# The decay mask of a recurrent attention kernel: its power computed in three pieces, and its semaphore waited for at the first use

## What is computed

```
q = xn @ Wq;  gate = softmax(xn @ Wg)
diff = s - t                                  # (512- to 1024-long causal pattern)
causal = diff > 0;  expn = max(diff - 1, 0)
for i in range(3):
    decay = sigmoid(decay_logits[i])          # logits 0, 3, 5
    w = decay ** expn * causal                # the decay mask
    scores = (q @ k_i.T) * w
    blended += gate[..., i] * (scores @ v_i)
y = x + (blended @ Wo * out_scale) * silu(ffn(xn))
```

## Time and profile before

| | |
|---|---|
| median of 3 runs | 1896.46 us (1894.89 to 1896.53) |
| the profiled execution's own time | 1895.22 us |
| its span, first to last instruction | 1893.2 us |
| mean granted clock of TensorE | 0.992 of full speed |
| busy, share of the span: TensorE, its weight loads | 97%, 66% |
| VectorE, GpSimd, ScalarE | 65%, 37%, 34% |
| chain that ended last | TensorE 92%, GpSimd 4%, the rest 1% or less each |

### The profile page before, as it was taken

How to read it: one execution, slowest core, us unless ns; L and a number is a source line. 1 busy time by engine, 2 the same in 40 slices (tenths; PEclk the granted TensorE clock), 3 DMA queues, 4 the chain that set the end, 5 groups by cost and what they waited for, 6 DMA issues and landing times.

```text
span 1893.2 us, 39454 instructions
## 1 busy us (share of the span) xinstructions
PE 1837.0 (97%) x14214; PEld 1249.3 (66%) x14214; DVE 1227.0 (65%) x2565; ACT 652.1 (34%) x1175; POOL 706.7 (37%) x641
## 2 busy tenths in 40 slices
PE   5786999999999999999999999999999999999999
PEld 1234848576685858677584857668585867758485
DVE  7773848576584838667484847658484856848374
ACT  2672414233332414243341423333242424334131
POOL 9393605234160614325060523416061432506021
PEclk9998999999999999999999999999999999999999
DMA  9962735566472746557373656647364654737350
GB/s 219 300 210 76 197 91 158 132 162 153 112 199 82 173 123 158 141 137 179 95 194 94 161 128 161 154 114 194 83 172 125 158 141 132 184 95 187 79 140 26
DMA packets 348662, 275.38 MB, mean 145 GB/s; under 512 B 216048, under 2 KB 253296, under 8 KB 348400
## 3 DMA queue, kind: packets, MB, share of 16 engines
q1 hardware_dynamic: 337664, 266.57, 53.7%
q0 software_dynamic: 10816, 6.30, 2.3%
HBM read 203.96 MB, written 30.54 MB: 124 GB/s over the span
## 4 chain that ended last, share of the span: by engine, by line
PE 92%; POOL 4%; DVE 1%; DMA 1%; issue 1%; SPq 1%; ACT 1%; POOLq 0%; DVEq 0%
PE F L1554 43%; PE F L1583 24%; PE B L1442 16%; POOL mask L668 3%; PE B L1474 2%; PE B L1447 2%; PE B L1449 2%; PE B L1448 2%; DVE region L1004 1%; PE F L1447 1%; PE F L1448 1%; PE F L1449 1%; DMA region<-in_wv 1%; SPq L519 0%; DMA lutrow<-in_lut 0%
## 5 line engine op out<-in xcount | busy, mean ns | idle before, releaser
L1554 PE MATMUL F<-xtc,ring 128*128 128x256 f16 (+1 forms) x4224 | 497.7, 273 | 0.0
L1554 PEld LDWEIGHTS F<-xtc,ring 128*128 128x128 f16 (+1 forms) x4224 | 416.0, 100 | 42.4
L1583 PE MATMUL F<-wd_hi,region 128*128 128x512 f16 (+1 forms) x1408 | 429.2, 379 | 0.0
L1554 PE MATMUL F<-xt,ring 128*128 128x256 f16 (+1 forms) x3168 | 378.8, 273 | 0.0
L1554 PEld LDWEIGHTS F<-xt,ring 128*128 128x128 f16 (+1 forms) x3168 | 309.9, 100 | 35.7 <-DVE region L1266 1.8
L1583 PE MATMUL F<-wd_lo,region 128*128 128x512 f16 (+1 forms) x704 | 266.7, 379 | 0.0
L1583 PEld LDWEIGHTS F<-wd_hi,region 128*128 128x128 f16 (+1 forms) x1408 | 137.5, 98 | 162.6
L684 POOL TENSOR_TENSOR rstd<-var,nhalf 128x4 f32<-128x4 f32 x15 | 15.3, 1019 | 595.3 <-DVE var L962 595.3
L1350 DVE SCALAR_TENSOR_TENSOR region<-F,row_out,region 128x512 f32<-128x512 f32 x64 | 48.0, 751 | 291.2 <-ACT region L931 291.2
L690 POOL TENSOR_TENSOR region<-region 128x512 f16<-128x512 f32 x96 | 121.6, 1267 | 220.9 <-ACT region L765 220.9
L931 ACT ACTIVATE region<-F,scale_hf 128x512 f32<-128x512 f32 x64 | 44.0, 687 | 435.5 <-PE F L1583 435.5
(11 more groups left out here) (200 smaller groups left out, 3069.9 us busy)
## 6 DMA issues: line engine op xcount, KB each, us to landing
ring<-blocks SPq DMA_DIRECT2D x546, 256.0 KB, 3.1
x_sb<-in_x SPq DMA_DIRECT2D x64, 256.0 KB, 3.5
out_y<-x_sb SPq DMA_DIRECT2D x64, 256.0 KB, 2.0
ring<-blocks SPq DMA_DIRECT2D x112, 128.0 KB, 2.5
blocks<-ring SPq DMA_DIRECT2D x35, 256.0 KB, 4.8
x_sb<-codes SPq DMA_DIRECT2D x10, 512.0 KB, 7.2
chalf<-codes SPq DMA_DIRECT2D x9, 512.0 KB, 7.1
xt<-codes SPq DMA_DIRECT2D x9, 512.0 KB, 9.0
```

The costliest lines, as they stand in the source:

```text
L1554: ins = T_.matmul(out_, a, b, start=fresh, stop=False, skip_group_check=True)
L1583: ins = T_.matmul(bf[:, :], a, b, start=(k == 0 and n == 0), stop=(k == FC - 1 and n == 2))
```

## The change

On GpSimd the iota and the maximum of the mask move up, directly behind `rstd`; the power over 128 x 384 becomes three powers over 128 x 128 (`power(0)`, `power(1)`, `power(2)`). The first stands in front of the sum over partitions, the other two behind the tables of powers. The wait for `s_dec` (the decays) moves up with the first. TensorE no longer waits for `s_mask`. VectorE waits for it in `probs_masked`, in front of every use, and no longer in front of its loop.

```diff
             pool.wait_ge(s_var, 2)
             G_.tensor_tensor(rstd[:, :], var[:, :], nhalf[:, :], ALU.pow).then_inc(s_rstd, 1)
-            pool.wait_ge(s_sq, 5)
-            G_.partition_all_reduce(gsum[:, :], amax[:, 0:5], P, RADD).then_inc(s_gsum, 1)
-
-            G_.iota(fade_s[:, :], ...)
-            G_.iota(fade_t[:, :], ...)
-            G_.memset(fade_tile[:, :], float(P)).then_inc(s_cstep, 1)
-            pool.wait_ge(s_dec, 3)
-            pool.wait_ge(s_cstep, 7)
-            for m in (fade_t, fade_s, fade_tile):
-                G_.tensor_tensor(m[:, :], decay[:, :], m[:, :], ALU.pow).then_inc(s_pow, 1)
...
             pool.wait_ge(s_mstep, 2)
             pool.wait_ge(s_pick, 2 * CG)
-            G_.tensor_tensor(mask[:, :, :], decay[:, :].unsqueeze(2).broadcast_to([P, NH, P]), mask_up,
-                             ALU.pow).then_inc(s_mstep, 1)
-            pool.wait_ge(s_mstep, 3)
+            pool.wait_ge(s_dec, 3)
+
+            def power(h):
+                G_.tensor_tensor(mask[:, h], decay[:, h:h + 1].broadcast_to([P, P]), mask_up[:, h],
+                                 ALU.pow).then_inc(s_mstep, 1)
+
+            power(0)
+            pool.wait_ge(s_sq, 5)
+            G_.partition_all_reduce(gsum[:, :], amax[:, 0:5], P, RADD).then_inc(s_gsum, 1)
+
+            G_.iota(fade_s[:, :], ...)
+            G_.iota(fade_t[:, :], ...)
+            G_.memset(fade_tile[:, :], float(P)).then_inc(s_cstep, 1)
+            pool.wait_ge(s_cstep, 7)
+            for m in (fade_t, fade_s, fade_tile):
+                G_.tensor_tensor(m[:, :], decay[:, :], m[:, :], ALU.pow).then_inc(s_pow, 1)
+
+            power(1)
+            power(2)
+            pool.wait_ge(s_mstep, 2 + NH)
             G_.affine_select(out=mask[:, :, :], in_=mask[:, :, :], compare_op=ALU.is_ge, fill=0.0,
                              **band).then_inc(s_mstep, 1)
...
             def probs_masked(gi, n):
 
+                dve.wait_ge(s_mask, 1)
                 dve.wait_ge(s_psc, gi * GT + n + 1)
...
-            dve.wait_ge(s_mask, 1)
             with dve.Fori(0, NB - 1) as i:
...
             pe.wait_ge(s_alo, len(MATS))
-            pe.wait_ge(s_mask, 1)
             with pe.Fori(0, NB - 1) as i:
```

More of the change, by code:

```diff
@@ L647, in _ @@
             G_.tensor_tensor(rstd[:, :], var[:, :], nhalf[:, :], ALU.pow).then_inc(s_rstd, 1)
+            band = dict(pattern=[[0, NH], [-1, P]], base=-1, channel_multiplier=1)
+            G_.iota(mask_up, allow_small_or_imprecise_dtypes=True, **band).then_inc(s_mstep, 1)
+            pool.wait_ge(s_mstep, 1)
+            G_.tensor_scalar(mask_up, mask_up, 0.0, None, ALU.max).then_inc(s_mstep, 1)
+            pool.wait_ge(s_mstep, 2)
+            pool.wait_ge(s_pick, 2 * CG)
+            pool.wait_ge(s_dec, 3)
[3 more added lines that the diff above has]
+            power(0)
             pool.wait_ge(s_sq, 5)
@@ L659, in _ @@
                 G_.tensor_tensor(m[:, :], decay[:, :], m[:, :], ALU.pow).then_inc(s_pow, 1)
[L662 to L667, removed]
-            G_.tensor_tensor(mask[:, :, :], decay[:, :].unsqueeze(2).broadcast_to([P, NH, P]), mask_up,
-                             ALU.pow).then_inc(s_mstep, 1)
-            pool.wait_ge(s_mstep, 3)
+            power(1)
+            power(2)
+            pool.wait_ge(s_mstep, 2 + NH)
             G_.affine_select(out=mask[:, :, :], in_=mask[:, :, :], compare_op=ALU.is_ge, fill=0.0,
                              **band).then_inc(s_mstep, 1)
-            pool.wait_ge(s_mstep, 4)
+            pool.wait_ge(s_mstep, 3 + NH)
             G_.tensor_scalar(mask[:, :, :], mask[:, :, :], 2.0 ** SP, None, ALU.mult).then_inc(s_mask, 1)
```

## The result

The changed kernel takes 1888.48 us, median of 5 runs (1887.88 to 1891.0); the kernel before 1896.53 in the same comparison. The ratio is 0.9959, 95% interval 0.9945 to 0.9974: faster by 8 us. The forecast was 1878.8 us, range 1875.5 to 1884: more than half of the gain that was forecast is missing. The profiled execution took 1887.88 us, its span is 1885.8.

A forecast was written before the change was run, and what follows sets the result against it. TensorE, 92% of the span, was taken to enter its loop late, waiting for GpSimd's mask. 18.15 - 2.2 (stall) + 1.7 (clock) = 17.65 us off 1895.22 gives 1877.6, as a median 1878.8; range 1875.5 to 1884.

The forecast's parts named there:

- TensorE's wait is removed: Entry of TensorE's loop: without the wait for the mask, the start moves from 156.46 to 138.31, by 18.15 us.
- The change of load in front of the sum: GpSimd, between power(0) and the sum over partitions: 8.3 us no longer hidden, so VectorE stalls 2.2 us.
- power(0): GpSimd's idle time behind `rstd`: the first power starts at 57.66, takes 21.1 us and ends at 78.8.
- The rival of unequal pieces: GpSimd's first power: head 0 might hold most of the 61.87 us, median up to 1919.6; chance 0.03.
- The rest of the mask: GpSimd behind the sum: tables 3.8 us as before, two powers of 21.1, mask ready near 144.6, nobody held.
- slack 21 us: Margin between the mask being ready near 144.6 and VectorE's first use of it at 165.4.
- the two signs: Either would make the prediction wrong: TensorE starting later than 143, or a first power other than 20 to 22 us.
- The port: Rival at the port GpSimd shares with VectorE: power(0) holds VectorE's compares for 21.1 us, median 1896; chance 0.02.
- TensorE's clock: First group's 96 matmuls: a shorter gap keeps the clock full, gaining 1.7 us, with 0 as other bound.
- the rival in which the clock falls all the same: TensorE's sparse last setup matmuls let the clock fall anyway: up to 1.7 us more, 1880.5; chance 0.12.
- VectorE's new wait: VectorE before each mask use, 64 times at 21 ns, 1.3 us in all: costed at nothing.

The follow-up runs named there:

- the waits alone: The kernel before with only the change's moved waits for the mask, GpSimd's order untouched: 1876.25 us, ratio 0.9896.
- VectorE's pause: The changed kernel, with VectorE also waiting for the three tables of powers in front of its unit 22: 1879.37 us, ratio 0.9906.
- three pieces at the old place: The kernel before with the change's moved waits and the power cut in three, one behind the other, where it stood: 1875.90 us, ratio 0.9894.
- the tables late: The kernel before with the change's moved waits, and GpSimd waiting for VectorE's unit 20 before the tables' iotas: 1911.05 us, ratio 1.0074.

## Why the prediction was wrong

- **TensorE's wait is removed: right.** 18.15 us without other shifts; 156.46 - 138.77 = 17.7 with the waits alone, which gained 20.9 us in the median; up to 1.6 us of it can be the clock's (18.45 against 20.08 for the 96 matmuls).
- **The change of load in front of the sum: right in kind, 0.9 too high.** It took 7.43 us (I took 8.3 from the way back), and the sum 0.46 instead of 1.25. VectorE stalled 0.7, not 2.2. VectorE's compares were not held by power(0) once it ran: eight beside it took 5.39 us, as in the earlier trace rows.
- **power(0): 21.9 us against 21.1**, right. In the four kernels that begin it at 56 to 58 us it took 20.8 to 22.7. The other two pieces took 20.7 each in the changed kernel, where nothing held them. The rival of unequal pieces is out.
- **The rest of the mask: this step failed.** "3.8 for the tables as before" was 36.7. I took the durations of the small instructions from the place where they had stood. There they ran beside VectorE's short steps on the scales (86.14 to 87.5). In the new order they come 10 us later, and the earlier trace rows say what stands there: VectorE busy 43.47 of 43.50 us. I read that row for TensorE's sake and not for GpSimd's. The mask was ready at 175.1 and not at 144.6, and "slack 21 us" became a wait of 8.4. Neither of the two signs by which I would have called the prediction wrong came: TensorE started before 143, and the first power lay within 20 to 22 us. The mask's time should have been the third.
- **The port: dismissed for the wrong direction.** The Trainium skill's "SBUF — State Buffer" (Who interferes with whom) says that whoever issues first gets the pair for the whole instruction, and the other blocks; and that an instruction of VectorE with two inputs collides with one of GpSimd that reads, not with one that only writes. I tested only whether GpSimd would block VectorE. The runs show the other direction, which was no rival of mine at all: VectorE's run of compares blocked GpSimd, 22.7 us for a three-column power. Of the rule the traces agree that GpSimd's start waits wholly for VectorE (22.68 us against 1.14), and that the iotas, which only write, end 0.12 us behind the start of one of VectorE's instructions with two inputs (101.53 and 101.41), beside which the power did not get through; they do not agree that the pair is held for a whole instruction of GpSimd, since 61.87 us of power ran beside compares of unchanged length (5.38 us for eight). That the thing held is the port is the Trainium skill's word; the runs show who waits for whom, and that the hold ends when the compares no longer overlap.
- **TensorE's clock: this term failed too, by 2.4 us.** I took a gain of 1.7 us. The 96 matmuls took 20.7 us, a loss of 0.6, and the wait for the mask brought a second stretch at 0.50. The clock had fallen in 137 to 138, before the last gap, so my reading by the length of that gap was of the wrong stretch; the rival in which the clock falls all the same came true. With the waits alone the start was half a microsecond earlier, after 1.19 us without a matmul, and the clock stayed up (18.45 us); with VectorE's pause it was again 1.19 us and the clock down (20.75); with three pieces at the old place again 1.19 us, and it fell only in 138 to 139 (0.82), when TensorE had resumed (20.13). The length of the last gap alone does not decide it. What does stays open; my bounds, 0 and 1.7, did not hold 20.7 against the 20.08 of before.
- **VectorE's new wait: nothing, right.** With it 64 times in the run, the waits alone reached the full forecast gain.

By its own terms: 1877.6 for the profiled execution; minus 1.2 for the earlier start, plus 2.4 for the clock at the start (20.7 against 18.3), plus 7.4 and 2.2 for the late mask and the clock behind it: 1888.4, measured 1887.88. The 2.2 was found as a remainder, so this shows that the pieces fit together and is no check of each.

## What to carry to other kernels

A duration belongs to a place: before an instruction is moved, look at what the engine that shares its port does at the new place, and in both directions. A wait in front of a loop is moved to the first use before anything else is rearranged; here that was the whole gain, and making the awaited work 6 us earlier was worth nothing. Short GpSimd work belongs where VectorE has gaps. One long instruction is safer than three, since only its start has to find an opening: cut in three at the old place, the mask was ready 6.4 us later, which here cost no time.

## What the runs showed of the hardware that I had not expected

- A run of VectorE's compares (128x2048, 16-bit, each 0.75 us and begun 0.66 us behind the last) holds off a GpSimd instruction that starts in its middle. A power over three columns took 22.7, 22.7 and 22.6 us in three kernels (the one behind it 11.35 in each), and 0.8 to 1.5 elsewhere; iotas took 6.4, 6.7 and 7.9 us in these three and 0.5 in the kernel before.
- The same compares a little apart (eight in 6.39 us instead of 5.39) let the same powers through in 0.9 to 1.5 us each.
- Once begun, a long power runs at its full rate beside them: 0.16 us a column either way (61.87 us beside them, 61.55 with the tables late, behind the last compare). Four pieces of 128 columns were held at their start, by 6 to 25 us, and came free at the short instruction over 12 columns or at the last compare. Why they did not come free at the longer ones of the same kind (0.75 and 1.82 us) is open, and so is why `fade_t` ended only at 124.35, when the next power had begun at 119.64.
- GpSimd's turn lasts too: in the kernel before its short instructions between 88 and 93 us went through amid the compares, having begun beside VectorE's short steps. There it was VectorE that lost, 1.3 us over twelve compares (3.01 and 6.42 us instead of 2.73 and 5.38). Why GpSimd kept its turn there is open.

```profile
87.53 3.01 DVE L1004 TENSOR_SCALAR region<-x_sb,code 128x2048 f16<-128x2048 f16 x4
90.46 6.42 DVE L1004 TENSOR_SCALAR region<-xt,code 128x2048 f16<-128x2048 f16 x8
```

- The change of what GpSimd has loaded costs 7.4 to 7.5 us in front of the sum and 7.1 to 8.4 behind it. The Trainium skill's GPSIMD Engine Reference (Instruction dispatch) has about 6 us at the first call; the trace agrees in kind, with 7.1 to 8.4 us, and has it at the change itself, where idle time can hide it: in the kernel before the sum began at 75.61, 0.14 us after ScalarE was done with the last square (75.47), and did not pay again.
